# Pacing GpSimd's row gathers by TensorE's node blocks in a GNN layer on one core

## What is computed

```python
edge_in_f = concat([h[src], h[dst], edge_features]);  msgs_f = relu(edge_in_f @ W1_f + b1_f) @ W2_f + b2_f
agg = segment_sum(msgs_f, dst)
edge_in_r = concat([h[dst], h[src], edge_features]);  msgs_r = relu(edge_in_r @ W1_r + b1_r) @ W2_r + b2_r
agg = agg + segment_sum(msgs_r, src)
out = x + h + relu(concat([agg, h]) @ Wn1 + bn1) @ Wn2 + bn2
```

## Time and profile before

| | us |
|---|---|
| median of 3 runs | 1574.19 |
| lowest, highest | 1571.79, 1575.95 |
| the profiled execution's own time | 1571.86 |
| its span | 1570.1 |
| PE, DVE, ACT, POOL busy | 1287.8, 971.1, 939.9, 1080.8 |

### The profile page before, as it was taken

One profiled execution on the slowest core, in us unless ns is written; L12 is line 12 of the kernel. 1 busy time (PEld: TensorE's weight loads), 2 busy tenths in 40 slices (PEclk: granted clock), 3 DMA queues, 4 the chain that ended last, 5 costly groups with the idle time before them and its releaser, 6 DMA issues.

```text
span 1570.1 us, 29474 instructions
## 1 busy us (share of the span) xinstructions
PE 1287.8 (82%) x7070; PEld 976.4 (62%) x7070; DVE 971.1 (62%) x3294; ACT 939.9 (60%) x2256; POOL 1080.8 (69%) x995
## 2 busy tenths in 40 slices
PE   5888989768877877778887778787778874999998
PEld 4777777556655665556665656665556653677776
DVE  7999999646666666666666666666666640222222
ACT  4888888545554555555454545554555533777776
POOL 8888888888888888888888888888888862000000
PEclk9999999787787788887787877888887786999999
DMA  6899998545555555555555555555555546999998
GB/s 215 303 312 314 319 311 308 169 90 108 108 110 111 112 102 104 105 99 103 104 106 106 105 105 101 102 102 107 106 104 102 103 79 176 382 372 370 362 365 295
DMA packets 238987, 281.00 MB, mean 179 GB/s; under 512 B 53747, under 2 KB 155777, under 8 KB 238925
## 3 DMA queue, kind: packets, MB, share of 16 engines
q1 hardware_dynamic: 168696, 241.57, 46.2%
q0 software_dynamic: 68992, 38.59, 20.3%
q10 hardware_dynamic: 1236, 0.30, 0.1%
HBM read 162.62 MB, written 117.72 MB: 179 GB/s over the span
## 4 chain that ended last, share of the span: by engine, by line
POOL 37%; issue 22%; PE 17%; DMA 3%; POOLq 1%; DVE 0%; ACT 0%; SPq 0%; DVEq 0%
POOL table L541 31%; POOL got_odd L523 6%; PE bank L888 6%; PE bank L899 6%; PE bank L909 3%; DMA table<-to_send,scatter_at 2%; DMA same<-table 1%; PE bank L863 1%; POOL got_even L523 0%; PE bank L837 0%; PE bank L835 0%; DVE same L996 0%; PE bank L850 0%; POOLq L539 0%; POOLq L119 0%
## 5 line engine op out<-in xcount | busy, mean ns | idle before, releaser
L541 POOL DMA_INDIRECT table<-to_send,scatter_at x392 | 621.0, 1584 | 133.0 <-issue 117.5
L863 PEld LDWEIGHTS bank<-message,same 128*128 128x128 f32 x1960 | 276.8, 227 | 43.2 <-issue 40.1
L863 PE MATMUL bank<-message,same 128*128 128x128 f32 x1960 | 297.9, 318 | 2.9 <-DVE message L1028 2.9
L656 ACT ACTIVATE nh<-nx,all_sums,all_rstd 128x64 f32<-128x64 f32 x784 | 280.2, 434 | 0.0
L523 POOL DMA_INDIRECT got_even<-in_x,gather_first x192 | 203.7, 1061 | 35.8 <-issue 35.8
L792 PE MATMUL bank<-wn_h,nturned 128*128 128x256 f32 x784 | 196.3, 394 | 29.3 <-ACT nhidden L700 24.4
L821 PE MATMUL bank<-ident,h_ends 128*128 128x128 f32 x196 | 53.3, 366 | 200.6 <-DVE h_ends L1037 200.6
L523 POOL DMA_INDIRECT got_odd<-in_x,gather_at x180 | 179.9, 999 | 54.8 <-issue 54.5
L996 DVE TENSOR_SCALAR_CACHE_REDUCE same<-others,ids 128x128 f32<-128x128 int32 (+3 forms) x392 | 190.7, 542 | 12.7 <-DVE ids L988 11.0
L792 PEld LDWEIGHTS bank<-wn_h,nturned 128*128 128x128 f32 x784 | 142.8, 192 | 65.4 <-issue 33.3
L1022 DVE TENSOR_TENSOR scatter_at<-moved,ids 128x4 int32<-128x4 f32 x98 | 15.9, 162 | 256.4 <-DMA table<-to_send,scatter_at 256.4
(11 more groups left out here) (81 smaller groups left out, 2000.3 us busy)
## 6 DMA issues: line engine op xcount, KB each, us to landing
nx<-in_x SPq DMA_DIRECT2D x194, 256.0 KB
table<-nhidden SPq DMA_DIRECT2D x97, 512.0 KB
same<-table SPq DMA_DIRECT2D x97, 512.0 KB, 5.3
others<-numbers SPq DMA_DIRECT2D x196, 128.0 KB
out_x<-nh SPq DMA_DIRECT2D x79, 256.0 KB, 4.4
nx<-out_x SPq DMA_DIRECT2D x55, 256.0 KB, 4.4
out_x<-ncentred SPq DMA_DIRECT2D x49, 256.0 KB, 4.2
table<-to_send,scatter_at POOLq DMA_INDIRECT x392
```

The lines of the kernel that those rows point to most:

```text
L541: pool.indirect_dma_start(table, bass.IndirectOffsetOnAxis(ap=scatter_at[s][:, k:k + 1], axis=0), to_send[s][:, k, :], None, compute_op=AL ...
L656: last = act.activation(nh[s][:, g, :], nx[place][:, g, :], ACT.Relu, bias=all_sums[:, at, g:g + 1].rearrange("p a g -> p (a g)"), scale=a ...
L863: last = pe.matmul(bank[6 + s][:, k * M:(k + 1) * M], same[s][:, o, k * P:(k + 1) * P], message[s][:, o, :], start=(o == k), stop=(o == KB ...
```

## The change

POOL's loop of the 208 gathers counts them in `gathers`. Ahead of gather n it calls `with_nodes(n)`: block `(n - 12) * 4 // 7` must have had its product (with 0 <= block < 98), so POOL waits on `b_product[block % 2]`. Gathers 0 to 11 have no wait, gathers 12 to 183 have one, and gathers 184 to 207 have none, because their block would be 98 or more. The memsets stay where they were. Nothing else changes.

```diff
     PAUSED = 200
+    AHEAD = 12
+    PACE = (7, 4)
     EARLY = 4
...
+            def with_nodes(n):
+                block = (n - AHEAD) * PACE[1] // PACE[0]
+                if 0 <= block < NW:
+                    pool.wait_ge(b_product[block % 2], block // 2 + 1)
+
             pool.wait_ge(s_begin, 2 * JT * 16)
-            pauses = 0
+            pauses = gathers = 0
             for b in range(NB):
...
                 for k in range(KB):
+                    if s == 0 or i < LOOK:
+                        with_nodes(gathers)
+                        gathers += 1
                     if s == 0:
                         gather(got_even[:, i, :], at, s_got_even[i >= EARLY], [k])
```

## The result

| | before | changed |
|---|---|---|
| median of 13 runs, us | 1574.15 | 1577.62 |
| lowest to highest | 1571.79 to 1577.12 | 1575.77 to 1581.53 |
| profiled execution, us | 1571.86 | 1579.84 |
| its span | 1570.1 | 1578.1 |

The ratio is 1.0028, 95% interval 1.002 to 1.0035: the change costs about 4 us (3.5 us between the medians). Ratios in this document leave out slow executions (over 1.5% above the fastest of their kernel), which occurred on one chip only, in the kernel before. Forecast were 1579.7 us (1573.5 to 1583.0) and, at 0.52, slower by over 0.3%. The time is in the range and the direction is right. The size was smaller: the ratio lies just inside the 0.3% that the prediction counts as no change.

The account below looks back on a forecast made before the run. POOL's queue, without reserve, was taken to bound the kernel. Satisfied waits added 0 and a recurring pause left a 5.5 us shift, put on the median of 1574.19: 1579.7 us, range 1573.5 to 1583.0.

Parts of the forecast that it names:

- What bounds the kernel: POOL's own queue, without reserve from the first scatter at 317.60 us on; any delay of its start there delays the end.
- Satisfied waits at 0: 172 added waits on POOL cost 0 when already satisfied; upper bound 0.02 us each, 3.4 us in all.
- Case E: POOL's node stage: satisfied waits cost over about 0.06 us each, +13 to +18 us (1587 to 1592); chance 0.07.
- The pause recurs at the same gather: POOL's unexplained 4.18 us stop after gather 140 comes again, so it stays 5.5 to 6.9 us late.
- rival A: The forecast itself: POOL's pause recurs late in the node stage, +5.5 to +6.9 us, 1579.7 to 1581.1; chance 0.44.
- Rival B: Without a pause, POOL's gathers are held to the last node product, +3.5 us, 1577.7, within 0.3%; chance 0.24.
- rival C: POOL's pauses come from gathers pressing on busy DMA engines; pacing removes them, 1575.4 us, +0.1%, not slower; chance 0.14.
- The first wait at gather 25: Node stage: gather 25, needing block 7, is the first too early, as TensorE stood still 5 us near 36 to 41.
- Node blocks and edge stage unchanged: DVE and TensorE keep their block time, and first scatter to end stays 1252.5 us, so the whole shift reaches the end.
- case D: Node blocks shorten, DVE's 8.2 us of idle time vanish: faster by 4.7 us (1569.5) or 2.8 (1571.4); chance 0.06.
- F: The added waits are always satisfied, so the change does nothing: 1574.2 us; chance 0.05.
- step 2: Unsatisfied waits in POOL's node stage: gather 140 must wait 6.79 us longer for block 73's product, the largest such gap.

Follow-up runs that it names:

- the other two: Against the kernel before, no added waits: memsets half as long, 1775.51 us; only the first memset and a fourth odd batch gathered ahead, 1809.87 us.
- the early waits: Changed kernel with only gathers 12 to 39 waiting for their block (28 of the 172 waits): 1577.85 us, ratio 1.0037 to the kernel before.
- the late ones: Changed kernel with only gathers 40 to 183 waiting for their block (144 of the 172 waits): 1577.20 us, ratio 1.0029 to the kernel before.

## Why the prediction was right, and where it was off

- **What bounds the kernel** held. A later first scatter reaches the end one to one: 1249.8 to 1254.3 us from the first scatter to the end in all 14 profiles, with the first scatter anywhere from 302.71 to 555.23 us (the 1249.8 is of the kernel with four gathers fewer behind it).
- **Satisfied waits at 0** held (ratio 1.0002). Case E is out.
- **The pause recurs at the same gather** held, in all 14 profiles. That was rival A's condition. Rival B (held to the last product) and rival C (pauses of pressure that pacing takes away) are out: in the changed kernel gather 182 comes 5.9 us behind the last product, and the pause is not shorter with the gate (4.96 and 5.03 us, against 3.73 to 4.51 without it, memsets in place). The measured median, 1577.62 us, is nevertheless rival B's number (1577.7) and not the forecast's: that agreement is chance, since what B describes did not happen.
- **The first wait at gather 25** held; the 5.5 to 6.9 us at the first scatter became 7.5 in the profiled pair. Gather 183 (290.67 us) and the first scatter (325.11 us) came just behind the stretches that the prediction gave for them, 285 to 290 and 321 to 324.5 us.
- **Node blocks and edge stage unchanged** held (last product 284.20 and 283.36 us, DVE busy 231.84 and 231.86): case D is out, and F too, as waits did end with products.
- **The term that was mis-sized is the lead of 6.79 us at gather 140** (step 2, unsatisfied waits). It came from one profile, that of the longest lead: five profiles in which no gate acted ahead of it have 6.8, 4.9, 6.8, 3.0 and 3.0 us, 1.9 us less on average. The sum then put this shift on top of the median of the runs (1574.19), while it belonged to an execution of 1571.86 us: a slower execution can already have lost part of the lead that the gate takes (of the five profiles without a gate there, the two with 6.8 us belong to the two fastest executions, 1571.35 and 1571.86 us). Put on its own execution it gives 1577.4 to 1578.8 us, which holds the measured 1577.62. The chance of 0.52 for slower by over 0.3% rested on the same step. The profiles themselves overstate the price (7.5 us): both profiled executions of the changed kernel lie above their medians, by 2.2 and 1.0 us. With two profiles of the changed kernel the size is not settled to better than 1 or 2 us: its first scatters are on average 6.5 us later than those of the five profiles without a gate ahead of gather 140, where the ratio gives 4.4 us.
- **What pacing is good for** was not in the prediction. Rival C named gathers pressing on the DMA engines and gave it little weight, as this profile shows no such pressure (share 0.93, DVE hardly idle). On one chip of those tried the kernel with a gate, and without memsets, took 1591.65 us; of those without a gate the kernel before took 1632.99 us at best, the other two 1775.51 and 1809.87.

## What to carry to other kernels

A gate on a queue that has no reserve costs the lead that it takes, once: here the early waits, the late ones and all together cost the same 4 to 6 us. Where something else takes the lead anyway, waits behind it cost next to nothing (the single one at gather 182). Make the gate's lead longer than the queue's greatest natural one, and it costs nothing (a lead of 18 gathers in place of 12 here). Read such a lead from more than one profile, and put a shift on the execution that it was read from, not on a median beside it. Fillers that space out a queue's work cost their full time as long as that queue sets the end, here down to a first scatter at some 305 us. A gate with a long lead cost nothing on the usual chips; that it would also hold the gathers on the odd one was shown for a lead of 12 only.

## What the runs showed of the hardware

- A gather that starts inside one of VectorE's two-input operations (L1098 and L1081, 0.69 us each) is stretched, so that it ends 0.84 us after that operation does. From 41 to 279 us the two profiled kernels have 85 gathers longer than 1.05 us (40 before, 45 changed). Every one began inside such an operation and ended 0.82 to 0.84 us after it. With a step of 1.39 us the gathers settle into seven in four blocks (10.7 us), two of them stretched, with and without a gate.
- A pause of 3.0 to 5.4 us stands ahead of the same gather in all 14 profiles: the second one of edge batch 64. The gather came at 194 us or at 242 us, as the 142nd gather or, with four odd ones more ahead of it, as the 146th:

```profile
190.21 0.95 POOL L525 DMA_INDIRECT got_even<-in_x,gather_first  x1 [0.30 <-issue]
194.50 0.95 POOL L525 DMA_INDIRECT got_even<-in_x,gather_first  x1 [3.35 <-issue]
```

  So it goes neither with the time nor with the number of gathers, memsets or waits before it, but with that gather. Against the number of gathers there is this one profile. Its cause stays open.
- On one of the chips, gathers at 1.26 us a step without a gate went with 45 GB/s and a DMA share of 0.18 in the node stage. On another chip the same step went with 318 GB/s, and on this one the DMA moved 304 GB/s behind a gate and 293 once the gathers were through. The mechanism was not shown.
